# Splitting the q/k weights on GpSimd, and the norm weight applied while an operand is copied

## The reference

```
qkvz = h @ W_qkvz                              # per key head: q, k, v (2 heads), z (2 heads)
q, k, v = silu(causal 4-tap convolution of each over time)
q, k = l2norm(q) / sqrt(128), l2norm(k)
step: S = a_t * S;  v_new = (v_t - S k_t) * b_t;  S = S + k_t v_new;  o_t = S q_t
og = o * silu(z)
og = og * rsqrt(mean(og * og) + eps) * norm_weight     # norm_weight: 128 numbers, one per feature of a head
out = og @ W_out                               # summed over all 32 value heads
```

## Time and profile before

| | us |
|---|---|
| median of 3 runs (lowest, highest) | 1398.95 (1396.54, 1399.48) |
| time of the profiled execution | 1393.76 |
| its span, first to last instruction | 1392.0 |
| PE busy in the span | 1225.8 (88%) |
| DVE busy | 944.0 (68%) |
| ACT busy | 820.1 (59%) |
| POOL busy | 723.4 (52%) |
| mean granted TensorE clock | 0.935 |

### The profile page before, as it was taken

The page is one execution under the profiler, slowest core; times in us unless marked ns, Lnnn a source line. Parts: engine busy times, 40 slices in busy tenths (PEclk is TensorE's granted clock), DMA queues, the critical chain, the costliest instruction groups (busy, mean ns, idle before and its releaser), DMA issues. The chain is left out here.

```text
span 1392.0 us, 30101 instructions
## 1 busy us (share of the span) xinstructions
PE 1225.8 (88%) x10608; PEld 1006.9 (72%) x10608; DVE 944.0 (68%) x2297; ACT 820.1 (59%) x2267; POOL 723.4 (52%) x1171
## 2 busy tenths in 40 slices
PE   7889999999999999999999899999987759988874
PEld 6787888888878788788878788888876645455553
DVE  6875879787887878787888778787722141134776
ACT  6344666676667676676766676666655323125871
POOL 3284666758585766857585866767571010020001
PEclk9776999999999999999999999999989677979997
DMA  4304031212214031312213041311202030000002
GB/s 162 91 17 104 16 91 31 76 39 70 56 51 102 10 99 25 82 36 72 48 60 102 6 103 23 85 35 35 51 1 60 1 93 0 0 1 1 2 2 95
DMA packets 138629, 70.69 MB, mean 51 GB/s; under 512 B 112456, under 2 KB 128336, under 8 KB 136560
## 3 DMA queue, kind: packets, MB, share of 16 engines
q1 hardware_dynamic: 138480, 68.78, 19.2%
HBM read 54.97 MB, written 13.76 MB: 49 GB/s over the span
## 5 line engine op out<-in xcount | busy, mean ns | idle before, releaser
L780 POOL TENSOR_TENSOR tmp<-Dm,Tn 64x31 f32<-64x31 f32 (+15 forms) x496 | 264.2, 533 | 89.7 <-DMA Dm<-blk_in_scratch 54.4
L783 POOL TENSOR_TENSOR Tn<-Tn,tmp 64x31 f32<-64x31 f32 (+15 forms) x496 | 281.7, 568 | 38.9
L618 DVE SCALAR_TENSOR_TENSOR cv<-bank,cw,cv 128x255 f32<-128x255 f32 (+2 forms) x384 | 155.2, 473 | 81.1 <-ACT cv L469 81.1
L756 POOL TENSOR_TENSOR ro<-ss,mhalf 128x4 f32<-128x4 f32 x64 | 64.5, 1008 | 242.2 <-ACT junk L531 209.5
L618 DVE SCALAR_TENSOR_TENSOR cqk<-bank,cw,cqk 128x255 f32<-128x255 f32 (+2 forms) x384 | 154.8, 472 | 7.5 <-ACT cqk L469 7.5
L397 PE MATMUL bank<-wo,OTs 128*128 128x256 f32 x512 | 139.1, 406 | 7.4 <-ACT OTs L561 7.4
L683 DVE SCALAR_TENSOR_TENSOR BP<-bank,cj,E 128x512 f32<-128x512 f32 (+1 forms) x256 | 142.7, 611 | 2.5 <-DVE cj L668 0.3
L531 ACT ACTIVATE junk<-og 128x129 f32<-128x129 f32 x256 | 79.8, 312 | 101.2 <-issue 87.5
L687 DVE TENSOR_TENSOR R<-Vs,bank 128x256 f32<-128x256 f32 x64 | 26.9, 421 | 137.4 <-PE bank L363 137.4
L397 PEld LDWEIGHTS bank<-wo,OTs 128*128 128x128 f32 x512 | 93.6, 198 | 22.8 <-ACT OTs L561 11.0
L539 ACT ACTIVATE ogn<-og,ro 128x128 f32<-128x128 f32 x256 | 81.9, 398 | 31.2 <-POOL ro L756 31.2
(11 more groups left out here) (210 smaller groups left out, 3523.7 us busy)
## 6 DMA issues: line engine op xcount, KB each, us to landing
rvz<-in_L_attn_W_qkvz SPq DMA_DIRECT2D x16, 512.0 KB, 5.4
x<-alpha_scratch SPq DMA_DIRECT2D x8, 1024.0 KB, 6.3
alb<-alpha_scratch SPq DMA_DIRECT2D x7, 1024.0 KB, 6.4
rqk<-in_L_attn_W_qkvz SPq DMA_DIRECT2D x16, 256.0 KB, 2.6
wo<-in_L_attn_W_out SPq DMA_DIRECT2D x16, 256.0 KB, 5.7
blk_in_scratch<-BP SPq DMA_DIRECT2D x256, 16.0 KB, 1.5
tinv_scratch<-Tn SPq DMA_DIRECT2D x32, 128.0 KB, 2.2
tinv_t_scratch<-Tt SPq DMA_DIRECT2D x32, 128.0 KB, 2.2
```

What stands on the lines that cost most here:

```text
L618: nc.vector.scalar_tensor_tensor(d, bk[:, t * T:(t + 1) * T - s], cw[p][:, first + t, TAPS - 1 - s:TAPS - s], d, ALU.mult, ALU.add).then_i ...
L780: pool_step_done(nc.gpsimd.tensor_tensor(t, Dm[:, j, j + 1:BLK].unsqueeze(2).broadcast_to([SLOTS, r, c]), Tn[:, j, 0:c].unsqueeze(1).broad ...
L783: pool_step_done(nc.gpsimd.tensor_tensor(Tn[:, j + 1:BLK, 0:c], Tn[:, j + 1:BLK, 0:c], t, ALU.subtract), kh * NTS + 2 * j + 4)
```

## The change

Two edits.

The low half of the q/k weights is no longer made by DVE at the end of step 1 but by POOL, in step 2, behind the `ro` of sequence 1 and in front of the third part of the inverse. The prologue's three splits stay where they are. The high half stays on ACT in step 1.

The rows of `wo` are no longer scaled: ACT applies `nw` in its copy of the turned outputs, where `nw` stands as a scale taken from SBUF, one per partition. The partition of the turned output is the feature of the head, the same index as the row of `wo`. PE then waits for the load of `wo` itself.

```diff
@@ pe_f
                     if b == 0:
-                        wait(nc.tensor, "wo_scaled", kh + 1)
+                        wait(nc.tensor, "wo_in", (kh + 1) * 16)
@@ act_ots
-                nc.scalar.activation(OTs[:].rearrange("p h c t -> p (h c t)"), bOT[:], ACT.Copy).then_inc(sem("ots"), 1)
+                wait(nc.scalar, "nw_scaled", 1)
+                nc.scalar.activation(OTs[:].rearrange("p h c t -> p (h c t)"), bOT[:], ACT.Copy, scale=nw[:, 0:1]).then_inc(sem("ots"), 1)
@@
-            def dve_wo(kh, p):
-                wait(nc.vector, "wo_in", (kh + 1) * 16)
-                wait(nc.vector, "nw_scaled", 1)
-                nc.vector.tensor_scalar(wo[p][:], wo[p][:], nw[:, 0:1], None, ALU.mult).then_inc(sem("wo_scaled"), 1)
-
@@ dve_step
-                if b == 0:
-                    dve_wo(kh, p)
...
-                splits(kh, p, b, dve_split_qk, dve_split_vz)
+                if b == 0 and kh and exists(kh + 1, 0, 0):
+                    dve_split_vz(kh + 1, 1 - p)
@@ pool_step
+            def pool_split_qk(kh, p):
+                wait(nc.gpsimd, "wqk_high", kh + 1)
+                nc.gpsimd.tensor_tensor(wqk[p][1][:], rqk[:], wqk[p][0][:].bitcast(F32), ALU.subtract).then_inc(sem("wqk_split"), 1)
+
...
+                    if b == 2 and exists(kh + 3, 0, 0):
+                        pool_split_qk(kh + 3, 1 - p)
                     pool_inverse(kh + 1, *SPLIT[b])
```

## The result

The changed kernel takes 1422.58 us as the median of 4 runs (1413.31 to 1424.72) against 1399.22 (1396.54 to 1401.17, 4 runs): a ratio of 1.0157, 95% interval 1.0116 to 1.0198. It is slower by some 23 us. The forecast was 1401.6 us, with a range of 1396 to 1409.

What follows compares the result with a forecast made beforehand. PE was taken to set the pace, held in step 3 by POOL's unbroken arc; +2.3 (split) - 0.2 (`wo` scaling) + 0.6 (`OTs` copy) = +2.7 us on the median 1398.95 gave 1401.6 us, range 1396 to 1409.

Steps and rivals of the forecast that it cites:

- What bounds the kernel: PE sets the pace; POOL's unbroken arc between the `ro` of sequences 1 and 2 makes it wait in step 3.
- The split taken from DVE: Ahead of sequence 1's scans and `og`: without the split, its `ro` starts 1.09 us earlier, read from turn 13.
- The split given to POOL: Head of POOL's arc: 1.24 us more, net +0.18 us a turn (+0.03 to +0.38); step 3's wait grows to 1.97.
- The scaling of `wo`: On DVE before step 0's scans: removing it saves 0 to 0.13 us a turn, -0.2 us taken in all.
- The copy to `OTs`: ACT's copy, 64 times: the scale adds 87 ns, mostly swallowed in steps 0 and 1; +0.6 us taken in all.
- The weight load that I named as cover: PE's last merge stage waits 30 times for ACT's `A`, 10.5 us in all, said to swallow most of the copy's delay.
- my 2.7: Sum of the terms over the whole kernel: +2.3 - 0.2 + 0.6 us.
- the nearer row: Profile row with the turning at full clock after 1.55 us idle; the other showed half clock after 3.05.
- rival 3: PE's clock falls to 1.2 GHz in step 3's longer wait, 2 us lost each turn, +26 us; chance 0.04.

Runs made afterwards that it cites:

- three pairs of kernels: Norm weight alone against the kernel before (0.17 us); both edits against only the split, with POOL's split in step 3 (0.23) or step 2 (0.29, falls taken off).
- the two pairs without falls: Norm weight alone (1394.83 us) against the kernel before; split on POOL in step 3 with the new norm weight (1388.13) against the old (1379.55).
- the filled kernels: The changed kernel with ten or three useless identity matmuls on PE ahead of the turning in step 3: 1398.53 us (ratio 1.0036) and 1398.9 us.
- the split alone: The changed kernel with the norm weight back in DVE's scaling of `wo`, so only the q/k split moves to POOL: 1406.34 us, ratio 1.0110 to the kernel before.
- the longer memset: The kernel before plus an unused 128x1024 memset on POOL ahead of the inverse's third part: 1419.41 us, against 1404.74 without it on that chip.
- the three traces that have them there: The changed kernel with the inverse dealt 9, 11, 11 (1408.86 us), the same with split in step 3 and old norm weight (1414.77), the changed kernel's third execution (1417.66).

## Why the prediction was wrong

**What bounds the kernel.** Right: PE's work is unchanged, and only its waits and its clock moved. The arc on POOL between the two `ro` has no idle time before or after the change and holds PE in step 3.

**The split taken from DVE.** Right: forecast -1.09 us from turn 13, measured -1.06. `ro` has 0.48 us of POOL's time to spare, as in the earlier trace rows. The wait for `Y` in step 2 is gone.

**The split given to POOL.** The instruction is as forecast (1.285 us against 1.269 in the earlier trace rows) and waits for nothing. The arc had 0.03 to 0.38 us of net growth, with +0.18 chosen; measured are 16.03 - 14.63 - 1.06 = +0.34. Most of the difference of 0.16 is what I couldn't see: at the end of step 2 the instructions of 175 and 156 elements now stand beside DVE's scans, and they take 1.03 and 0.71 us where they took 0.51 and 0.44. Before, it was a later pair, of 156 and 135 elements, that took 0.75 and 0.68 where it now takes 0.48 and 0.41, so what is left is some 0.25 us in turn 4 and 0.15 in the mean. (The engines, then, meet at more than semaphores.) At the split's own place nothing was hit: DVE stood idle from 405.59 to 406.89 us, waiting for PE. Wait forecast 1.97, measured 2.14.

**The scaling of `wo`.** Worth nothing that shows; DVE now waits for PE at `nrm`, as forecast (0.31 us in turn 4).

**The copy to `OTs`.** +87 ns forecast, +92 measured. But little of it is swallowed: the turn is 0.17 to 0.29 us longer in three pairs of kernels, at or above the bound of 2 x 0.087 and not near the 0.04 I took. The weight load that I named as cover waits as before, 10.5 us in all, so the delay went by it. By the two pairs without falls (0.17 and 0.23) this term should have been some +2.5 for 13 turns, not +0.6. The pairs also differ in DVE's scaling of `wo`, and the times of the runs don't resolve a term of this size.

**The sum without the clock.** 0.52 us a turn by the filled kernels, 6.8 us for 13 turns against my 2.7. That would have made 1406, inside the range.

**The clock.** This is the step that failed: the sum had no term for the clock. I wrote that at full clock stands "the nearer row", 1.55 us, and gave the fall a chance of 0.04. The rows held 1.55 and 3.05, the latter from step 1 of turn 14; my wait of 1.97 lay between them, and no row said anything of the gap. The Trainium skill, TensorE: Matmul & The Clock Gate, section The HAM clock gate, ties the fall to an idle stretch longer than this one. The runs contradict it as I read it: waits of 2.1 us in step 3 bring the fall in 8 to 12 turns of 12, in step 1 waits of 1.61 and of 1.14 us each stood in front of one, and 1.74 in step 3 never did. The mechanism of rival 3 was what happened, with a size that I put too high: one fall costs 1.35 us of a turn (11.97 against 10.62), not 2. 12 falls make 16 us. With the 6.8 us of the edits that is 23, close to the trace's 22.75 us over turns 1 to 12. That the medians differ by nearly the same (23.4) is in part luck: the profiled pair differs by 19.5, and no execution of some 1422 us was seen in a trace.

The proof doesn't rest on the trace of the change alone. Matmuls that compute nothing take the fall away with the edits in place, and a memset brings it without them.

## What to carry to other kernels

Before work is moved to an engine with idle time, look at where that time lies: POOL was half idle, yet one arc of it ran unbroken, and PE waited at its end. The same 1.3 us on POOL cost 1.1% there (the split alone, most of it by the clock), and the move from DVE gained 1.1% with the split placed some 14.5 us later in the turn. And where a change lengthens a regular wait of the matmul engine, price the clock too, over the whole gap between the longest wait known to be harmless and the shortest known to hurt, taken at the same place in the kernel; if the new wait falls into that gap, the range has to hold both.

## What the runs showed of the hardware

Behind the waits of some 2.1 us in step 3 the clock falls at most 1.3 us after the turning has begun, and stays at its lower level for 3.4 us. In the trace of the change the turning still runs at full speed in every turn (0.66 us). In others the fall comes sooner: with the split alone the turning of turn 1 takes 1.11 us, with the longer memset that of turn 7 takes 1.12. Equal waits of 2.13 us end in a fall or not from one turn to the next, so near this length the time of a kernel scatters by 1.35 us for each turn. The falls in step 1 lasted three times as long or more: 10.2 us in the window shown, and they cost 3.2 to 4.5 us each in turns 1 to 12 of the three traces that have them there. POOL's short instructions take longer beside DVE's scans: 1.03 instead of 0.51 us at 64x175. And an ACT copy from PSUM with a per-partition scale from SBUF took 92 ns more than one without at 128x512 (684 against 592), and 87 at 128x256.
